# Slot rows kept group by group, counts stored one source tile at a time, and SyncE's count work moved seven chunks behind its loads

## What is computed

```python
q, k, v = (h[src] @ qW), (h[dst] @ kW), (h[dst] @ vW)          # layer 0, 4 heads
scores = clip(einsum('ehd,ehd->eh', q, k), -10, 10)
w = exp(scores) / (segment_sum(exp(scores), src)[src] + 1e-8)
x = x + h + segment_sum(w * v, src)
# layer 1: a softmax over incoming edges; layer 2: ten propagation steps
# with the normalized adjacency; layer 3: two graph convolutions
```

## Time and profile before

| | us |
|---|---|
| median of 3 runs (4158.35 to 4160.02) | 4158.38 |
| the profiled execution, its own time | 4161.24 |
| its span, first to last instruction | 4159.8 |
| the 245 chunks, first L996 to last L996 | 279.9 to 1188.6 |

### The profile page before, as it was taken

How to read it: one execution, slowest core, us unless ns; L and a number is a source line. 1 busy time by engine, 2 the same in 40 slices (tenths; PEclk the granted TensorE clock), 3 DMA queues, 4 the chain that set the end, 5 groups by cost and what they waited for, 6 DMA issues and landing times.

```text
span 4159.8 us, 127348 instructions
## 1 busy us (share of the span) xinstructions
PE 3900.6 (94%) x46212; PEld 3670.6 (88%) x46212; DVE 1814.7 (44%) x4407; ACT 1428.1 (34%) x4491; POOL 517.5 (12%) x708
## 2 busy tenths in 40 slices
PE   3779999999979998999999999999999999979898
PEld 2669999999965655999999999999999999979898
DVE  8988999999983223222222222222222222251211
ACT  1247787777771001222222222222222222220100
POOL 1015555555530000000000000000000000000000
PEclk9989999999989999999999999999999999989999
DMA  1029999999973332566656656666565666556574
GB/s 39 3 66 218 220 223 221 220 217 221 220 193 109 107 108 90 183 203 205 202 201 204 205 200 202 204 203 200 203 205 202 201 204 204 174 176 206 161 214 138
DMA packets 525172, 746.04 MB, mean 179 GB/s; under 512 B 203503, under 2 KB 449647, under 8 KB 525036
## 3 DMA queue, kind: packets, MB, share of 16 engines
q1 hardware_dynamic: 520040, 743.21, 60.9%
q10 hardware_dynamic: 4996, 0.88, 0.1%
HBM read 620.51 MB, written 83.32 MB: 169 GB/s over the span
## 4 chain that ended last, share of the span: by engine, by line
PE 70%; DVE 10%; SPq 7%; issue 5%; DMA 5%; ACT 1%; POOL 1%; DVEq 0%; ACTq 0%; POOLq 0%
PE sum L1588 48%; PE sum L1333 14%; PE sum3a L1333 4%; DMA rows<-slot_rows_d 4%; SPq L956 3%; DVE onerank L755 2%; SPq L963 1%; SPq L952 1%; SPq L939 1%; POOL sc L1059 1%; DVE sc L989 1%; DVE qk L982 1%; PE pk L1107 1%; DVE bt L727 1%; DVE prodb L744 1%
## 5 line engine op out<-in xcount | busy, mean ns | idle before, releaser
L1588 PE MATMUL sum<-y,ring 128*128 128x192 f16 x12005 | 994.7, 246 | 4.3 <-ACT y L1490 4.3
L1588 PEld LDWEIGHTS sum<-y,ring 128*128 128x128 fp8e4 x12005 | 993.5, 98 | 4.9 <-issue 4.5
L1588 PE MATMUL sum<-u2b,ring 128*128 128x192 f16 x12005 | 991.2, 246 | 0.0
L1588 PEld LDWEIGHTS sum<-u2b,ring 128*128 128x128 fp8e4 x12005 | 990.5, 98 | 0.0
L1333 PE MATMUL sum<-u,ring 128*128 128x385 f16 (+1 forms) x4802 | 614.0, 288 | 31.5 <-ACT u L1458 22.2
L1596 DVE TENSOR_TENSOR z<-lo,sum 128x96 f32<-128x96 f32 x490 | 124.5, 254 | 1120.0 <-ACT lo L1611 1119.5
L1333 PEld LDWEIGHTS sum<-u,ring 128*128 128x128 fp8e4 x4802 | 435.8, 98 | 200.1 <-issue 38.0
L1107 PE MATMUL pk<-kv,hT 128*128 128x192 f16 x4900 | 486.1, 247 | 11.7 <-DVE hT L1001 9.5
L1107 PEld LDWEIGHTS pk<-kv,hT 128*128 128x128 f16 x4900 | 409.7, 99 | 13.2 <-DVE hT L1001 9.6
L1611 ACT ACTIVATE lo<-sum 128x96 f32<-128x96 f32 x490 | 123.1, 251 | 747.4 <-PE sum L1588 747.4
L1188 ACT ACTIVATE kvs<-pk 128x384 f32<-128x384 f32 x735 | 313.6, 437 | 153.8 <-PE pk L1107 148.7
(11 more groups left out here) (248 smaller groups left out, 3180.1 us busy)
## 6 DMA issues: line engine op xcount, KB each, us to landing
ring<-adjacency_t SPq DMA_DIRECT2D x490, 800.0 KB, 4.3
ring<-adjacency SPq DMA_DIRECT2D x147, 896.0 KB, 4.8
rows<-slot_rows_d SPq DMA_DIRECT2D x245, 320.0 KB, 4.1
adjacency<-row SPq DMA_DIRECT2D x147, 128.0 KB, 3.6
adjacency_t<-col SPq DMA_DIRECT2D x147, 128.0 KB, 2.7
adjacency<-row SPq DMA_DIRECT2D x49, 256.0 KB, 3.7
adjacency_t<-col SPq DMA_DIRECT2D x49, 256.0 KB, 2.4
adjacency<-row SPq DMA_DIRECT2D x49, 160.0 KB, 3.7
```

The source lines that it names most:

```text
L1588: m = pe.matmul(ps[r][:, 0:2 * D], w[:, t // 2, :, t % 2], U[:, t, 0:2 * D], start=t == 0, stop=t == TILES - 1)
```

## The change

Four edits.

1. `slot_rows_d` is laid out `[tile, group, 2, 128]` where it was `[tile, 2, 25 * 128]`. A chunk's numbers are now one contiguous piece of 2560 bytes in DRAM where they were two of 1280.
2. `rows` takes the same order, `[P, 5, 2, 128]` for `[P, 2, 640]`, so that the load is one run for each partition. L996 and L1001 now read `rows[h][:, :, 0, :]` and `rows[h][:, :, 1, :]`: five rows of 128 with gaps of 128 between them. `hT` is declared `[P, 3, 5, 128]`, which is the same memory as before. In the built program the output of L996 and L1001 is still one run of 640, and the input, one run of 640 before, is now written as 5 rows of 128 at a pitch of 256.
3. Each tile's counts are stored by one DMA of 800 KB (`store`), and the transposed ones by one of 800 KB (`store_turned`), where each chunk had its own of 128, 160 or 256 KB. The transposes (`turn_counts`) stay one for each chunk. The semaphores go by tile (`b`) where they went by chunk.
4. On SP the transposes are done 7 chunks behind the loads (`SENT`), with `store` behind a tile's last; `store_turned` is 9 chunks behind (`SP_LAG`). Before it was 3, 3 and 5.

```diff
-            to = k.rows_d.rearrange("(x t) i (g e) -> t i g x e", t=2, e=P)
+            to = k.rows_d.rearrange("(x t) g i e -> t i g x e", t=2)
...
-    rows = [k.buf(ctx, f"rows{i}", [P, 2, CHUNK * P], F16) for i in range(HOMES)]
+    rows = [k.buf(ctx, f"rows{i}", [P, CHUNK, 2, P], F16) for i in range(HOMES)]
...
-    hT = [k.buf(ctx, f"hT{i}", [P, 3, CHUNK * P], F16) for i in range(2)]
+    hT = [k.buf(ctx, f"hT{i}", [P, 3, CHUNK, P], F16) for i in range(2)]
...
-    LAG = 5
+    LAG, SENT, SP_LAG = 5, 7, 9
...
-        src = k.rows_d[2 * X + b, :, at:at + CHUNK * P]
-        sp.dma_start(rows[i][:], src.partition_broadcast(P)).then_inc(k.rows_in[i].sem, 16)
...
+        src = k.rows_d[2 * X + b, g0:g0 + CHUNK, :, :].rearrange("g i e -> (g i e)")
+        sp.dma_start(rows[i][:].rearrange("p g i e -> p (g i e)"), src.partition_broadcast(P)).then_inc(k.rows_in[i].sem, 16)
+
+    def turn_counts(X, e):
+
+        b, u = e // CHUNKS, units(e)
+        g0, g1 = u[0][1], u[-1][1] + u[-1][2]
+        if e % CHUNKS == 0:
+            sp.wait_ge(k.col_out[b].sem, k.col_out[b].at(X, -1))
+            k.settle(sp)
+        sp.wait_ge(k.out_c.sem, k.out_c.at(X, u[-1][0]))
         k.settle(sp)
...
+        sp.dma_start_transpose(col[b][:, g0:g1, :], flat(row[b][:, g0:g1, :])).then_inc(k.row_out[b].sem, 16)
+
+    def store(X, b):
+
+        sp.dma_start(k.c_d[2 * X + b, :, :], flat(row[b][:]).bitcast(U8)).then_inc(k.row_out[b].sem, 16)
+
+    def store_turned(X, b):
+        sp.wait_ge(k.row_out[b].sem, k.row_out[b].at(X, 16 * CHUNKS + 15))
         k.settle(sp)
...
+        sp.dma_start(k.t_d[2 * X + b, :, :], flat(col[b][:]).bitcast(U8)).then_inc(k.col_out[b].sem, 16)
...
-        for x, e in lagged(X, c, 3, first, chunks):
-            send(x, e)
-        for x, e in lagged(X, c, 5, first, chunks):
-            send_transposed(x, e)
+        for x, e in lagged(X, c, SENT, first, chunks):
+            turn_counts(x, e)
+            if e % CHUNKS == CHUNKS - 1:
+                store(x, e // CHUNKS)
+        for x, e in lagged(X, c, SP_LAG, first, chunks):
+            if e % CHUNKS == CHUNKS - 1:
+                store_turned(x, e // CHUNKS)
...
-        v.tensor_scalar(hT[i][:, 0, :], rows[h][:, 0, :], k.pid[:, 0:1], None, ALU.is_equal)
+        v.tensor_scalar(hT[i][:, 0, :, :], rows[h][:, :, 0, :], k.pid[:, 0:1], None, ALU.is_equal)
...
-            t = v.tensor_scalar(hT[i][:, 1 + m, :], rows[h][:, 1, :], k.dpid[:, m:m + 1], None, ALU.is_equal)
+            t = v.tensor_scalar(hT[i][:, 1 + m, :, :], rows[h][:, :, 1, :], k.dpid[:, m:m + 1], None, ALU.is_equal)
...
-        a.wait_ge(k.row_out[c].sem, k.row_out[c].at(X, 32 * b - 1))
+        if c == 0:
+            a.wait_ge(k.row_out[b].sem, k.row_out[b].at(X, -1))
```

More of the change, by code:

```diff
@@ L879, in attention_signals @@
     k.ratio, k.totalled = (Beat(k, f"at_{x}", 2) for x in ("ratio", "totalled"))
-    k.row_out, k.col_out = ([Beat(k, f"at_{x}{c}", n) for c in range(CHUNKS)] for x, n in (("row_out", 64), ("col_out", 32)))
+    k.row_out, k.col_out = ([Beat(k, f"at_{x}{b}", n) for b in range(2)] for x, n in (("row_out", 16 * CHUNKS + 16), ("col_out", 16)))
     k.out_c = Beat(k, "at_out_c", 2 * UP)
@@ L934, in load_rows @@
     def load_rows(X, e):
-        b, i, at = e // CHUNKS, e % HOMES, (e % CHUNKS) * CHUNK * P
+        b, i, g0 = e // CHUNKS, e % HOMES, (e % CHUNKS) * CHUNK
         sp.wait_ge(k.turned.sem, k.turned.at(X, e - HOMES))
         k.settle(sp)
-        src = k.rows_d[2 * X + b, :, at:at + CHUNK * P]
-        sp.dma_start(rows[i][:], src.partition_broadcast(P)).then_inc(k.rows_in[i].sem, 16)
-    def parts(e):
-        u = units(e)
-        return e // CHUNKS, u[0][1], u[-1][1] + u[-1][2], u[-1][0]
@@ L946, in send @@
[L946 to L950, removed]
-        k.settle(sp)
-        sp.dma_start(k.c_d[2 * X + b, :, g0 * GROUP:g1 * GROUP],
-                     flat(row[b][:, g0:g1, :]).bitcast(U8)).then_inc(k.row_out[c].sem, 16)
-        sp.wait_ge(k.col_out[c].sem, k.col_out[c].at(X, 16 * b - 1))
-        k.settle(sp)
-        sp.dma_start_transpose(col[b][:, g0:g1, :], flat(row[b][:, g0:g1, :])).then_inc(k.row_out[c].sem, 16)
@@ L1106, in take @@
                 for part in range(2):
-                    t = pe.matmul(pk[(3 * e + n) % 2][:, place:place + 2 * D], hT[i][:, 1 + m, g * P:(g + 1) * P],
+                    t = pe.matmul(pk[(3 * e + n) % 2][:, place:place + 2 * D], hT[i][:, 1 + m, g, :],
                                   k.kv[:, 2 * (g0 + g) + m, part, :], start=m == part == 0, stop=m == part == 1)
@@ L1118, in query @@
             for part in range(2):
-                t = pe.matmul(pq[:, g * D:(g + 1) * D], hT[i][:, 0, g * P:(g + 1) * P], q2[b][:, part, :],
+                t = pe.matmul(pq[:, g * D:(g + 1) * D], hT[i][:, 0, g, :], q2[b][:, part, :],
                               start=part == 0, stop=part == 1)
@@ L1210, in scalar_step, with paired @@
                 copy_q(x, e // CHUNKS)
-    def paired(eng, step):
-        for c in range(LAG):
+    def paired(eng, step, lag=LAG):
+        for c in range(lag):
             step(0, c, first=True)
         with eng.Fori(0, PAIRS - 1) as X:
-            for c in range(LAG, CP):
+            for c in range(lag, CP):
                 step(X, c)
-            for c in range(LAG):
+            for c in range(lag):
                 step(X + 1, c)
-        for c in range(LAG, last_chunks + LAG + 1):
+        for c in range(lag, last_chunks + lag + 1):
             step(PAIRS - 1, c, chunks=last_chunks)
@@ L1243, in vector @@
         v.tensor_tensor(k.most[:], most[:, 0:1], most[:, 1:2], ALU.max).then_inc(k.most_s.sem, 1)
-    vector(), paired(pool, gpsimd_step), paired(pe, tensor_step), paired(a, scalar_step), paired(sp, sync_step)
+    vector(), paired(pool, gpsimd_step), paired(pe, tensor_step), paired(a, scalar_step), paired(sp, sync_step, SP_LAG)
     for e in (v, a, pe, pool, sp):
-        for s in k.col_out:
-            e.wait_ge(s.sem, s.at(PAIRS - 1, 16 * last_tiles - 1))
+        for b in range(2):
+            e.wait_ge(k.col_out[b].sem, k.col_out[b].at(PAIRS - 1 if b < last_tiles else PAIRS - 2, 15))
         e.wait_ge(k.normed.sem, k.normed.at(PAIRS - 1, last_tiles - 1))
@@ L2097, in gnn @@
         v, a, pe, pool, sp = k.v, k.a, k.pe, k.pool, k.sp
-        k.rows_d = nc.dram_tensor("slot_rows_d", [BTILES, 2, GROUPS * P], F16).ap()
+        k.rows_d = nc.dram_tensor("slot_rows_d", [BTILES, GROUPS, 2, P], F16).ap()
         k.c_d = nc.dram_tensor("adjacency", [BTILES, P, WIDE], U8).ap()
```

## The result

The changed kernel takes 4166.91 us (median of 20 runs, 4165.69 to 4167.86), the one before 4159.35 in the same session: ratio 1.0018, 95% interval [1.0011, 1.0024]. It is slower by 7.6 us, where 176 were forecast. Its profiled execution has a span of 4165.8 us, 6.0 more than before, and the same number of instructions.

What follows compares the result with a forecast made beforehand. No engine was far from its limit, so the order of events decided. Slower comparisons (+0.50) and the `hd` stall (+0.81) made 4.43 us a chunk against 3.72: +173, with the tail +176, 4334 us; range 4120 to 4370.

Steps and rivals of the forecast that it cites:

- `wv` goes in front of `hd`: POOL's `wv` asks in the middle of `hs`, so DVE's `hd` takes 1.29 for 0.48: +0.81 us in every chunk.
- The rate: DVE's L996 and L1001 fall to half rate, about 0.54 us each: +0.50 us a chunk for three instructions.
- `sc` and L994 freed of POOL: Slower comparisons no longer exclude POOL: `sc` mostly near 0.36 us, not 0.84, and the source comparison no longer spread.
- Where `wv` asks: On POOL, `wv` asks 1.00 us behind the reduction's end, in the middle of DVE's `hs`.
- `wv` asks at the same point each time: The state holds itself: PE waits for `qk`, so ACT's exponent is never late and `wv`'s asking stays constant.
- The forecast's sum: Plain chunk 4.13 us, a tile's first 5.47, a tile 22.16 or 4.43 a chunk: +173 us, +176 with the tail.
- Rival 1: No new collision of `wv` with `hd` though the rate halves: 3.62 us a chunk, 4137 us; chance 0.14.
- The wait for rows: L996's 67 us of waits for loads go; POOL is late next, so 0.15 a chunk, -37 us.
- the tile of gapless chunks: A tile without row waits: 5.18 + 2.82 + 3 x 3.23 + 0.17 = 17.86 us, 3.57 a chunk against 3.72.
- The tail: At the end, two whole-tile stores follow the last transpose and PE's last wait ends later: +3 us, between +1 and +8.
- Rival 3: Comparisons on DVE fall to one element a cycle, +0.50 us each: 5.11 a chunk, +339, 4497 us; chance 0.06.

Runs made afterwards that it cites:

- e8: Kernel of e5 with the source comparison (L994) alone given a one-run input and a 5-row output: 4143.62 us, ratio 0.9961 to the kernel before.
- e3: Changed kernel with a gap of two elements behind each group of `hT`, so the comparisons' output is 5 rows like the input: 4193.23 us, ratio 1.0081.
- e14: Changed kernel with one tiny write (a memset of one column) on DVE ahead of the two destination comparisons, no wait added: 4314.35 us.
- e4: Changed kernel with one more wait on DVE, so that `hd` waits until the `hs` just ahead has finished: 4315.28 us, ratio 1.0372.
- e6: Changed kernel with two tiny writes on DVE and a wait that they need, ahead of `hs`: 4314.97 us, ratio 1.0373.
- e9: Changed kernel with two tiny writes on DVE and a wait that they need, ahead of the two destination comparisons: 4314.31 us, ratio 1.0361.
- e11: Kernel of e9 with the clip of `sc` widened from 20 to 80 columns, to make `wv` ask later: 4316.25 us, ratio 1.0371.
- e12: Changed kernel with one tiny write on DVE and a wait that it needs, ahead of `hs`: 4313.36 us, ratio 1.0362.
- e1: Changed kernel with the old layout of the slot rows, so only SP's new order and stores are in: 4153.79 us, ratio 0.9991 to the kernel before.
- e5: Kernel of e1 with the last tile's counts stored in two parts each, the last unit alone at the end: 4152.05 us, ratio 0.9981.

## Why the prediction was wrong

The direction was right. The size was not, and one step made it so: "`wv` goes in front of `hd`". That the direction came out is in part luck: the collision that was to bring it did not come, and the small loss is what is left of other terms that nearly cancel.

- **The rate: right.** 0.54 us was forecast for each comparison, 530 ns measured. The Trainium skill's rule ("Vector Engine (DVE) Microarchitecture Reference", §5.1) holds here in both directions: input 5 rows against output one run, 530 ns; input one run against output 5 rows, 535 (e8). With 5 rows on both sides 403 (e3).
- **`sc` and L994 freed of POOL: right.** `sc` 0.35, L994 with no spread.
- **Where `wv` asks: right once in a tile.** 1.00 behind the end of the reduction was forecast, and 0.99 is measured in the first plain chunk. "`wv` asks at the same point each time" was wrong: it asks at 1.09, 1.45 and 2.02 in the next three. That constancy holds only in the state forecast, where `hd` is held (0.99 in all four in e14).
- **"and goes in front of `hd`": this step failed.** It was +0.81 in every plain chunk, 158 of the 173 us of the stage. Measured, `hd` takes 0.48 in all plain chunks: it passes a `wv` that already waits (1.58 and 1.48 long) in two of four, and in the other two `wv` asks too late to hold it. The forecast's sum nearly holds once that one thing is as it said: e4, e6, e9, e11, e12 and e14 have a plain chunk of 4.1 us and 4313 to 4316 us, where the forecast had 4.13 and 4334. Their pace is 4.33 (e14) against 4.43, mostly because a tile's first chunk is shorter than the 5.47 of the sum (5.13 from 536.67 to 541.80 in e14). The rows of before held the sign that was overlooked: `sc` at 546.91 in the earlier trace rows asks while the first L1001 runs, and lasts 0.84, so it also stood behind the second. It ends 0.07 behind the end of `hs` (547.68), as the `sc` of e3 ends 0.06 behind that of `hd`, so `hs` probably passed it too. A waiting POOL was passed there, and the source line of L1059 before says that it was the rule (the middle figure is the median, in ns):

```profile
L1059 POOL TENSOR_SCALAR sc<-sc,bound x245: 357/842/849, 287.4 to 1195.9; 128x20 f32<-128x20 f32 x123
```

  I read the 0.84 as "held by L1001" and drew from the one row at 543.98, a tile's first chunk, that the engine that waits goes first. The rule that the Trainium skill gives ("SBUF — State Buffer", § Who interferes with whom: whoever issues first has the shared pair for the whole instruction) doesn't say who goes next when one already waits. "First asked, first served" was my own addition.
- **Rival 1 named the right state and missed its point.** It gave 4137 for "no new collision" and let it hang on whether `wv` asks before 1.25 behind the reduction. In the first two plain chunks it does, and there is no collision. Its price was too low as well: the collision in a tile's first chunk stays (5.25 us from `qk` to `qk`, where rival 1 had 4.66), a plain chunk is 3.29 where it had 3.32, and the last of a tile takes 3.59; the pace is 3.73 and not 3.62.
- **The wait for rows: mis-sized.** Gone as forecast (67 us to 4.7), but worth 12 us (e1), not 37: the tile of gapless chunks left out the wait for `kvs` in its last chunk, 0.56 us, whose cause (TensorE takes the tile's sums, then ScalarE's copy) stood at the end of the earlier trace rows as 0.30.
- **The tail: right.** +3, between +1 and +8, was forecast; the verdict is 1.9 later against the last reduction and 4.5 in all. e5 shows that splitting the stores takes 1.3 us of it back.
- **Two slips in the sums.** Rival 3's +339 is 1.39 x 244 and leaves out the tail that it names. The tail's own sum starts at 1195.5, a transpose issued 0.3 earlier than in the earlier trace rows, without saying that the store ahead of it is gone.

The groups of DVE in the changed kernel's stage, to set beside e1's, whose L999 has a mean of 381, `hd` 640 and `hs` 479:

```profile
L999 DVE TENSOR_SCALAR hT<-rows,dpid 128x640 f16<-128x640 f16 x488 | 240.0, 530 | 0.0
L980 DVE TENSOR_TENSOR qk<-pq,kvs 128x480 f32<-128x480 f32 x243 | 157.1, 646 | 7.6 <-ACT kvs L1187 4.3
...
L1030 DVE TENSOR_TENSOR hd<-high_d,low_d 128x640 bf16<-128x640 bf16 x244 | 136.0, 557 | 0.0
L1026 DVE TENSOR_TENSOR hs<-count,ss 128x640 bf16<-128x640 bf16 x244 | 134.8, 553 | 0.0
L994 DVE TENSOR_SCALAR hT<-rows,pid 128x640 f16<-128x640 f16 x244 | 129.5, 531 | 4.7 <-DMA rows<-slot_rows_d 4.7
```

What the layout does to a mean chunk, from e1 to the changed kernel: two L999 +0.30, `hs` +0.07, L994 -0.16, `hd` -0.08, the waits of `qk` (28.8 us to 7.6) -0.09. The sum is +0.04, the measured pace +0.06 (3.675 to 3.733). So the halved rate costs 0.48 a chunk in the three comparisons' own time against an uncontended 0.37, and most of it comes back, since L994 no longer waits for `wv` and `qk` hardly waits for `kvs`. In all, -12 us for the loads and +14 for the layout make +2 in the stage; 1.9 for the tail and 1.5 behind the verdict bring the profiled spans to +6.0. The medians differ by 7.6; the profiled execution of the kernel before was itself 1.9 above its median.

## What to carry to other kernels

When two engines exclude each other, look for a row in which one that waits is passed, before you say who goes first: a short operation that lasts as long as two of the other engine's is such a row. A slower form of an instruction can be worth taking where it leaves a shared port free (L994 in e8), and isn't where the engine is already the limit. And a wait that is removed is worth only the way to the next one: lay out the whole cycle, a tile here, with each engine's chain, not the typical chunk alone. The same holds for a collision: if it doesn't come in the first chunk, the moments of the following chunks move.
